# Mamba layer: y summed by channels on TensorE, dt read from its bank, six of sixteen states' dt·u·B made by TensorE

## The chip, the cores and the metric

One core of one Trainium2 chip runs the whole program. The time is device microseconds of one execution; runs agree within some 0.5%, and the kernel before was timed three times. The engines are TensorE (PE, with its weight loads in a row of their own, PEld), VectorE (DVE), ScalarE (ACT), GpSimd (POOL) and SyncE (SP, which only issues DMAs here). Each engine works through its own instructions in order and waits on semaphores that the others count up.

## The reference, cut to what matters

The program is one layer: a bidirectional Mamba block over 8 sequences of 512 tokens with 128 model channels, then attention and a mixture of experts. Only the Mamba block is touched. For each sequence and each of the two directions (256 inner channels, 16 states):

```
u, z = split(x @ Win.T);  u = silu(conv4(u) + convb)
dtr, B, C = split(u @ Wx.T)                     # 8, 16, 16 wide
dt = softplus(dtr @ Wdt.T + bdt)
h[n] = exp(dt * A[n]) * h[n] + (dt * u) * B[n]  # over 512 tokens, for each of 16 states n
y = sum over n of h[n] * C[n]  + u * D
out = (y * silu(z)) @ Wout.T
```

The backward direction runs the same on the flipped sequence and flips the result.

## The kernel before, in words

Everything of the scan lies by channels: 128 channels on the partitions, 512 tokens in the free dimension, so that the 256 channels are two halves h = 0, 1. One (sequence b, direction d) is a unit: 16 units in a row, written as a first unit, a loop over pairs of units (d = 1 of a sequence, then d = 0 of the next) and a last unit. A unit has 32 steps s, with state n = s // 2 and half h = s % 2. At each step:

- ACT makes `da = exp(dt * A[n])` into a ring of 8 (`act_da`, L722).
- DVE multiplies `dtu = dt*u` with the row B[n] spread over the partitions, which TensorE puts into a bank of `bp` by a bf16 matmul (`pe_b`, L479): `dbu`, L866. Then it scans (`dve_scan`, L882).
- POOL multiplies the scanned row with C[n] spread over the partitions: `hc`, L1025, a ring of 8.
- TensorE adds it up (`pe_y`, L491): four transposes of 128x128 add the 512 tokens of `hc` into `yp`, which lies by tokens. The same happens once for u·D (`ud`).

For four states of a unit (`BY_PE`) TensorE makes dtu·B itself, by matmuls of the transposed dtu (`pe_dtt`, L440, copied by ACT into `dtt`) with diagonal matrices of B, which ACT writes (`act_diag`, L690): `pe_fill`, L454, one call for each half. The scan then reads that bank.

While a unit scans, the other work of its neighbours is done in the same steps. The front of the next unit: the convolution as 8 matmuls (`pe_u`, L402), z (`pe_z`, L411), Wx (`pe_xd`, L420), Wdt (`pe_dt`, L470), B transposed (`pe_bt`, L428), softplus on ACT as Abs, Relu, Exp, Ln (L702 to L710) and the sum on DVE (`dve_dt`, L852), then dtu (L857). The tail of the unit before: the last five `pe_y`, then y·silu(z) on DVE (`dve_yg`, L889), TensorE transposes that back to channels (`pe_ygt`, L508), ACT copies it (`act_ygt`, L730), and Wout follows once for both directions (`pe_out`, L514), with its end on DVE (L897 to L911).

The order on each engine is written out by hand: `pe_unit`, `act_unit`, `dve_unit` and `pool_unit` run over s and call what is due. A "slot s" of TensorE below is one turn of the loop in `pe_unit`: in odd slots the B row or the first half's fill of state s//2 + 1, in even slots the second half's fill of state s//2 - 1, then the y of step s - 5 (`LAG_Y`), then tail and front. A unit with direction 1 carries the tail of direction 0 and has no `pe_out`; it is called A here. A unit with direction 0 carries the tail of direction 1 with `pe_out`; it is called B.

After the 16 units (at about 990 us) attention and experts run in a part of the program that is left as it was.

Of the kernel before, what the change touches and what calls it, by code (L numbers as in the profile page):

```python
# [18 lines left out]
ALU = mybir.AluOpType  # L19
# [57 lines left out]

FIRST_IN = (2, 4)
# [12 lines left out]
BY_PE = ((2, 4, 12, 14), (2, 4, 6, 14))  # L91
N_PE = len(BY_PE[0])
DIAG_AT = ((-1, 5, 18, 20), (-1, 5, 11, 20))
# [20 lines left out]
def mamba_phase(nc, sems, shared, x, x1, cscr, w, ffn):  # L114

    with ExitStack() as ctx:
# [30 lines left out]
        sz = part(NDIR, TC, DI)  # L147
        yg = part(TC, DI)
# [11 lines left out]
        eps = shared["wt"][:, taken:taken + TC]  # L160
        q9, k9 = shared["q9"], shared["k9"]
# [6 lines left out]
        ncol = sb("ncol", [P, 2])  # L168
# [37 lines left out]
        lnw = ncol  # L206
# [41 lines left out]
        ygt_ready = sig("ygt_ready", 4, "tensor")  # L248
# [20 lines left out]
        dt_done = sig("dt_done", 4, "vector")  # L269
# [17 lines left out]
                   (late_loaded, wu[:, 1], w["tap_w"][:, 1]), (late_loaded, wout[...], w["wout"]))  # L287

# [12 lines left out]
        def sp_first_load(sp):  # L301
# [9 lines left out]
            sp.dma_start(lnw[:, :], ffn["lnw"]).then_inc(ffn_loaded, 16)  # L311
# [77 lines left out]
        def pe_u(pe, b, d, i, first=False):  # L389
# [53 lines left out]
        def pe_fill(pe, b, d, n, h):  # L443
# [9 lines left out]
            for c in range(TC):  # L453
                last = nc.tensor.matmul(dst[:, c * P:(c + 1) * P], dtt[:, c, h * P:(h + 1) * P], diag[:, (N_PE * d + e) % 2, c, :],  # L454
# [26 lines left out]
        def pe_y(pe, b, d, s):  # L481
# [14 lines left out]
        def pe_ygt(pe, b, d, last_unit=False):  # L496
            pe.wait_ge(yg_done, count(yg_done, b, d + 1))
            if last_unit:
                pe.wait_ge(ygt_done, count(ygt_done, b, 2))
                pe.wait_ge(res_done, count(res_done, b, 0))  # L500
                pe.wait_ge(first_rope, 4)
            elif d:
                pe.wait_ge(dtt_done, count(dtt_done, b + 1, 2))
            else:
                pe.wait_ge(dtt_done, count(dtt_done, b, 4))
            for h in range(NH2):
                for c in range(TC):
                    last = nc.tensor.transpose(wp[:, h, c * P:(c + 1) * P], yg[:, c, h * P:(h + 1) * P], ident[:, :])  # L508
                last.then_inc(ygt_ready, 1)

        def pe_out(pe, b, c):
            pe.wait_ge(ygt_done, count(ygt_done, b, 4))
# [18 lines left out]
        def pe_unit(pe, b, d, front=None, tail=None, after=None):  # L531


            for s in range(STEPS):
# [21 lines left out]
                if tail and s == 7:  # L556
                    pe_ygt(pe, *tail)
# [8 lines left out]
                if front:  # L566
# [18 lines left out]
        def _(pe):  # L585
# [58 lines left out]
        def act_silu_z(act, b, d, k):  # L644
            act.wait_ge(z_ready, count(z_ready, b, 2 * d + k + 1))
            if k == 0:
                act.wait_ge(yg_done, count(yg_done, b, d - 1))
            h = k ^ d
            nc.scalar.activation(sz[:, d, 2 * h:2 * h + 2, :], wp[:, h, :].rearrange("p (c n) -> p c n", c=2),
                                 ACT.Silu).then_inc(silu_done, 1)  # L650

        def act_xd(act, b, d, k):
# [5 lines left out]
            elif k == 1:  # L658
# [4 lines left out]
                nc.scalar.activation(xd[:, :], wp[:, d, :], ACT.Copy).then_inc(xd_done, 1)  # L663
# [2039 lines left out]
```

## Time and profile before

| | us |
|---|---|
| three runs | 1722.72, 1725.72, 1731.79; median 1725.72 |
| the profiled execution | 1706.65, span 1704.9 |
| Mamba part | first scan at 38.9, last scan at 976.6 |
| DVE busy over the span | 1385.4 (81%) |
| PE busy over the span | 1323.4 (78%) |
| POOL, ACT busy over the span | 1109.9 (65%), 1062.2 (62%) |

Busy shares are means over the Mamba part and the part behind it. A row of a timeline gives start, duration, engine, line, operation, tiles and shapes, how many instructions stand in the row, and in brackets the idle time before it with what ended it. A matmul's duration holds its pipeline's tail, so what one costs TensorE in a dense stretch is the distance from its start to the start of the next row. One matmul of the program in f32 leaves two records, one f32 transpose of 128x128 leaves one.

### The profile page before, as it was taken

Reading aid. Unit: us, or ns where it says so; the run is one execution under the profiler, and the core shown is the slowest. Engines: PE = TensorE matmul, PEld = TensorE weight load, DVE = VectorE, ACT = ScalarE, POOL = GpSimd, SP = SyncE. Lnnn points to the kernel's source line nnn. Section 1 sums busy time; section 2 is a strip of 40 time slices with the busy share of each in tenths; the row PEclk is TensorE's granted clock in tenths of the full one; section 3 lists DMA queues with packets and bytes.
Section 4 is the critical chain, followed back from the end, with each engine's and each line's share of the span. In section 5 each row is a group of like instructions: output and inputs, shape, how many; then the busy total and the mean of one; then the engine's idle time right before and its main releaser. Section 6 shows DMA issues by size and latency. Waiting matters only on the chain. (4 is left out here: it accounts for less than half of the span.)

```text
span 1704.9 us, 30907 instructions
## 1 busy us (share of the span) xinstructions
PE 1323.4 (78%) x8880; PEld 958.7 (56%) x8880; DVE 1385.4 (81%) x2234; ACT 1062.2 (62%) x1888; POOL 1109.9 (65%) x1244
## 2 busy tenths in 40 slices
PE   4877788787778777877877658888988888888771
PEld 2656566566656665665666433335665556656671
DVE  2999999999999999999999846676778777777432
ACT  6777777776786776777867315565665656556330
POOL 1777777787877777777868814444557566655535
PEclk8989998899889899898998757898999999999886
DMA  5112302320321123023203021134556455564662
GB/s 190 54 59 101 125 1 99 124 99 4 121 99 61 64 99 124 0 99 124 81 19 141 27 89 30 50 125 134 175 152 200 149 173 168 155 198 134 224 221 72
DMA packets 115274, 186.05 MB, mean 109 GB/s; under 512 B 10736, under 2 KB 87536, under 8 KB 110960
## 3 DMA queue, kind: packets, MB, share of 16 engines
q1 hardware_dynamic: 111056, 176.30, 29.9%
q0 software_dynamic: 4096, 8.40, 1.7%
q8 instruction: 44, 0.72, 0.2%
q14 instruction: 78, 0.64, 0.1%
HBM read 153.92 MB, written 26.15 MB: 106 GB/s over the span
## 5 line engine op out<-in xcount | busy, mean ns | idle before, releaser
L882 DVE TENSOR_TENSOR_SCAN wt<-da,dbu 128x512 f32<-128x512 f32 x448 | 527.6, 1204 | 17.4 <-ACT da L722 6.8
L722 ACT ACTIVATE da<-dt,a_neg 128x512 f32<-128x512 f32 x512 | 351.4, 716 | 186.2 <-DVE wt L882 161.4
L1025 POOL TENSOR_TENSOR hc<-wt,qk 128x512 f32<-128x512 f32 x256 | 327.8, 1299 | 97.2 <-DVE wt L882 75.3
L1025 POOL TENSOR_TENSOR hc<-wt,cb 128x512 f32<-128x512 f32 x256 | 326.1, 1294 | 93.0 <-DVE wt L882 87.9
L491 PE MATMUL yp<-ident,hc 128*128 128x128 f32 x2048 | 321.8, 291 | 5.4 <-POOL hc L1025 5.1
L2018 ACT ACTIVATE pt<-scores,lift 128x512 f32<-128x512 f32 x320 | 216.3, 684 | 167.3 <-PE scores L1761 165.8
L491 PEld LDWEIGHTS yp<-ident,hc 128*128 128x128 f32 x2048 | 271.9, 153 | 84.6 <-issue 52.2
L2149 DVE TENSOR_REDUCE mx<-wp 128x1 f32<-128x384 f32 (+3 forms) x352 | 217.9, 635 | 91.3 <-PE wp L1723 86.9
L866 DVE TENSOR_TENSOR dbu<-dtu,bp 128x512 f32<-128x512 f32 x384 | 251.4, 684 | 10.9 <-PE bp L479 1.0
L2496 POOL TENSOR_SCALAR_AFFINE_SELECT pt<-pt 128x256 f32<-128x256 f32 (+1 forms) x320 | 119.0, 375 | 190.1 <-ACT pt L2018 189.0
L402 PE MATMUL wp<-xpad,wu 128*128 128x512 f32 x256 | 132.5, 610 | 11.6 <-DVE wt L897 6.5
L1723 PE MATMUL wp<-qk 72*128 72x384 bf16 (+3 forms) x512 | 136.1, 324 | 0.0
L1761 PE MATMUL scores<-qk 75*128 75x384 bf16 (+3 forms) x512 | 130.6, 317 | 3.4 <-ACT pt L2018 3.4
L1720 PE MATMUL wp<-mask,identb 128*128 128x128 bf16 (+2 forms) x352 | 91.3, 259 | 32.5 <-DVE mx L2149 26.5
L1780 PE MATMUL og<-pt,vpad 128*32 128x512 f32 (+3 forms) x1024 | 98.3, 482 | 23.0 <-POOL pt L2496 23.0
L440 PE MATMUL wp<-ident,dtu 128*128 128x128 f32 x128 | 31.5, 427 | 79.7 <-DVE dtu L857 79.7
L2516 POOL DMA_INDIRECT yk<-ys_scratch,pos_e x64 | 61.8, 966 | 45.6 <-DMA ys_scratch<-ysb 30.7
L479 PE MATMUL bp<-st,sel 96*128 96x512 bf16 x192 | 78.8, 410 | 10.3 <-DVE dbu L866 9.6
L1761 PEld LDWEIGHTS scores<-qk 75*128 75x128 bf16 x512 | 48.7, 102 | 64.0 <-ACT pt L2018 32.1
L454 PE MATMUL dbu<-diag,wt 128*128 128x128 f32 x512 | 71.1, 282 | 16.4 <-DVE wt L882 16.4
L454 PEld LDWEIGHTS dbu<-diag,wt 128*128 128x128 f32 x512 | 64.4, 193 | 33.3 <-DVE wt L882 26.0
L690 ACT ACTIVATE diag<-ident,bt 128x128 f32<-128x128 f32 x256 | 81.2, 389 | 1.6
(252 smaller groups left out, 2441.9 us busy)
## 6 DMA issues: line engine op xcount, KB each, us to landing
wt<-ffn_w_e SPq DMA_DIRECT2D x120, 384.0 KB, 4.4
qk<-c_scratch SPq DMA_DIRECT2D x8, 3072.0 KB, 11.6
cb<-c_scratch SPq DMA_DIRECT2D x8, 3072.0 KB, 11.8
qk<-q_scratch SPq DMA_DIRECT2D x96, 96.0 KB
qk<-c_scratch SPq DMA_DIRECT2D x8, 1024.0 KB, 4.7
cb<-c_scratch SPq DMA_DIRECT2D x8, 1024.0 KB, 4.7
xg<-xs_scratch SPq DMA_DIRECT2D x24, 256.0 KB, 3.4
ys_scratch<-ysb SPq DMA_DIRECT2D x24, 256.0 KB, 3.0
```

Source lines behind the costliest of these rows:

```text
L402: last = nc.tensor.matmul(wp[:, h, :], wu[:, d, j, h * P:(h + 1) * P], xpad[:, d, j:j + SEQ], start=(j == 0), stop=(j == NTAP - 1))
L454: last = nc.tensor.matmul(dst[:, c * P:(c + 1) * P], dtt[:, c, h * P:(h + 1) * P], diag[:, (N_PE * d + e) % 2, c, :], start=True, stop=True)
L491: last = nc.tensor.matmul(yp[:, c, h * P:(h + 1) * P], src[:, c * P:(c + 1) * P], ident[:, :], is_transpose=True, start=(s < 0 and h == 0 ...
L722: nc.scalar.activation(da[:, s % NDA, :], dt[:, h, :], ACT.Exp, scale=a_neg[:, d, h, n:n + 1]).then_inc(da_done, 1)
L866: nc.vector.tensor_tensor(dbu[:, dbu_bank(d, n) ^ h, :], dtu[:, h, :], bp[:, n % 2, :], ALU.mult).then_inc(dbu_done, 1)
L882: nc.vector.tensor_tensor_scan(hb[:, s % NHB, :], da[:, s % NDA, :], src, 0.0, ALU.mult, ALU.add).then_inc(scan_done, 1)
L1025: nc.gpsimd.tensor_tensor(hc[:, s % NHC, :], hb[:, s % NHB, :], cb[d][:, s // 2, :], ALU.mult).then_inc(hc_done, 1)
L1723: last = nc.tensor.matmul(heads[:, i, :], q9[0:PART_ROWS, at, h0_ % GH + i, c * P:(c + 1) * P], k9[0:PART_ROWS, at, 0:width], start=False, ...
L1761: last = nc.tensor.matmul(sp_[:, t % 2, at:at + SEQ - kc * P], k9[:, group, kc * P:(kc + 1) * P], q9[:, group, h % GH, kc * P:], start=Tru ...
L2018: nc.scalar.activation(pt[:, (ST_TILES * b + t) % NPR, 0:width], scores_in, ACT.Exp, bias=lift[:, :], scale=SCALE).then_inc(exp_done, 1)
L2149: nc.vector.reduce_max(mx[:, c, h:h + n], ms[:, t % 2, 0:n * (c + 1) * P].rearrange("p (n k) -> p n k", n=n), mybir.AxisListType.X).then_i ...
L2496: nc.gpsimd.affine_select(out=found, in_=found, pattern=[[0, len(pieces(t))], [1, P]], base=0, channel_multiplier=-1, compare_op=ALU.is_ge ...
```

## The change

Five things are done together.

1. `yp` now lies by channels. `pe_y` is one f32 matmul of 512 columns with the identity as weights, in place of four transposes; `dve_yg` writes `ygt` directly (for direction 1 backwards), and `pe_ygt` and `act_ygt` go. `sz` lies by channels too, for which `pe_z` is one matmul of 512 columns per half in place of two of 256.
2. `BY_PE` has six states in both directions (2, 4, 6, 8, 12, 14) in place of four, with four buffers of diagonals in place of two and the diagonals written at other steps.
3. The bias of dt comes with the matmul, by a row of ones in `xd`; ACT's Relu goes, and DVE makes max(., 0) + ln(.) of each half straight from the bank, in steps 28 and 29.
4. B is transposed in slot 24 between the two `pe_dt`, not in slot 30, and copied in ACT's step 29.
5. Waits follow these edits; those on `ygt_done` become waits on `dtt_done` or `yg_done`.

```
-BY_PE = ((2, 4, 12, 14), (2, 4, 6, 14))
+BY_PE = ((2, 4, 6, 8, 12, 14), (2, 4, 6, 8, 12, 14))
...
-DIAG_AT = ((-1, 5, 18, 20), (-1, 5, 11, 20))
+DIAG_AT = ((-1, 4, 8, 12, 17, 21), (-1, 4, 8, 12, 17, 21))
...
+        yp = shared["yp"][:, :, :].rearrange("p c n -> p (c n)").rearrange("p (h s) -> p h s", h=NH2)
...
         def pe_z(pe, b, d, k):
             pe.wait_ge(silu_done, count(silu_done, b, 4 * d + k + 1))
             h = k ^ d
-            for c in (2 * h, 2 * h + 1):
-                last = nc.tensor.matmul(wp[:, h, (c % 2) * DI:(c % 2 + 1) * DI],
-                                        xpad[:, d, NTAP - 1 + c * P:NTAP - 1 + (c + 1) * P], win_z[:, d, :],
-                                        start=True, stop=True)
-            last.then_inc(z_ready, 1)
+            nc.tensor.matmul(wp[:, h, :], win_z[:, d, h * P:(h + 1) * P], xpad[:, d, NTAP - 1:NTAP - 1 + SEQ],
+                             start=True, stop=True).then_inc(z_ready, 1)
...
         def pe_dt(pe, b, d, h):
...
+            else:
+                pe.wait_ge(bt_done, count(bt_done, b, d + 1))
...
             for h in (range(NH2) if s < 0 else (s % 2,)):
                 src = ud[:, h, :] if s < 0 else hc[:, s % NHC, :]
-                for c in range(TC):
-                    last = nc.tensor.matmul(yp[:, c, h * P:(h + 1) * P], src[:, c * P:(c + 1) * P], ident[:, :],
-                                            is_transpose=True, start=(s < 0 and h == 0 and c % 2 == 0),
-                                            stop=(s == STEPS - 1), skip_group_check=True)
+                last = nc.tensor.matmul(yp[:, h, :], ident[:, :], src, start=(s < 0), stop=(s >= STEPS - NH2),
+                                        skip_group_check=True)
             last.then_inc(y_added, 1)
...
-                if tail and s == 7:
-                    pe_ygt(pe, *tail)
...
-            act.wait_ge(fill_done, count(fill_done, b, N_PE * d + e - 1))
+            act.wait_ge(fill_done, count(fill_done, b, N_PE * d + e - 3))
...
-                nc.scalar.activation(t_relu[:, h, :], wp[:, 1 - (h ^ d), :], ACT.Relu, bias=bias).then_inc(soft_done, 1)
...
-                nc.vector.tensor_tensor(dt[:, :, :], t_ln[:, :, :], t_relu[:, :, :], ALU.add).then_inc(dt_done, 1)
...
+                nc.vector.scalar_tensor_tensor(dt[:, k, :], wp[:, 1 - (k ^ d), :], 0.0, t_ln[:, k, :],
+                                               ALU.max, ALU.add).then_inc(dt_done, 1)
...
-            dve.wait_ge(ygt_ready, count(ygt_ready, b, 2 * d))
-            nc.vector.tensor_tensor(yg[:, :, :], yp[:, :, :], sz[:, d], ALU.mult).then_inc(yg_done, 1)
+            dve.wait_ge(out_ready, count(out_ready, b, 0))
+            out = ygt[:, d]
+            nc.vector.tensor_tensor(out[:, :, ::-1] if d else out, yp, sz[:, d], ALU.mult).then_inc(yg_done, 1)
```

TensorE, first unit (direction 0), from the work on state 6 in slot 11 on. `bp<-st,sel` is a B row, `bp<-diag,wt` or `dbu<-diag,wt` a fill, `wp<-xpad,wu` the convolution, `yp` the sum over states. Before:

```order
L479 MATMUL bp<-st,sel 128x512
L491 MATMUL yp<-ident,hc 128x128 x8
L402 MATMUL wp<-xpad,wu 128x512
L479 MATMUL bp<-st,sel 128x512
L491 MATMUL yp<-ident,hc 128x128 x4
L402 MATMUL wp<-xpad,wu 128x512
L491 MATMUL yp<-ident,hc 128x128 x4
L402 MATMUL wp<-xpad,wu 128x512
L479 MATMUL bp<-st,sel 128x512
L491 MATMUL yp<-ident,hc 128x128 x4
```

The same place of the same engine now:

```order
L455 MATMUL bp<-wt 128x128 x4
L493 MATMUL yp<-hc,ident 128x512 x2
L407 MATMUL wp<-xpad,wu 128x512
L482 MATMUL bp<-st,sel 128x512
L493 MATMUL yp<-hc,ident 128x512
L407 MATMUL wp<-xpad,wu 128x512
L455 MATMUL dbu<-wt 128x128 x4
L493 MATMUL yp<-hc,ident 128x512
L407 MATMUL wp<-xpad,wu 128x512
L455 MATMUL bp<-wt 128x128 x4
L493 MATMUL yp<-hc,ident 128x512
L407 MATMUL wp<-xpad,wu 128x512 x2
```

The B rows of states 6 and 8 have become two fills each, and each group of four transposes is one matmul of 512 columns.

DVE, first unit, from the first scan of state 4 to state 9. `L882` and `L862` are the scans (the listing names them by their instruction's class), `L866` and `L846` the products. Before:

```order
L882 SCALAR_TENSOR_TENSOR wt<-da,bp 128x512
L866 TENSOR_TENSOR dbu<-dtu,bp 128x512
L882 SCALAR_TENSOR_TENSOR wt<-da,dbu 128x512
L866 TENSOR_TENSOR dbu<-dtu,bp 128x512
L882 SCALAR_TENSOR_TENSOR wt<-da,dbu 128x512 x2
L866 TENSOR_TENSOR dbu<-dtu,bp 128x512 x2
L882 SCALAR_TENSOR_TENSOR wt<-da,dbu 128x512 x2
L866 TENSOR_TENSOR dbu<-dtu,bp 128x512 x2
```

Now:

```order
L862 SCALAR_TENSOR_TENSOR wt<-da,bp 128x512
L846 TENSOR_TENSOR dbu<-dtu,bp 128x512
L862 SCALAR_TENSOR_TENSOR wt<-da,dbu 128x512
L846 TENSOR_TENSOR dbu<-dtu,bp 128x512
L862 SCALAR_TENSOR_TENSOR wt<-da,dbu 128x512 x2
L862 SCALAR_TENSOR_TENSOR wt<-da,bp 128x512
L846 TENSOR_TENSOR dbu<-dtu,bp 128x512
L862 SCALAR_TENSOR_TENSOR wt<-da,dbu 128x512
L846 TENSOR_TENSOR dbu<-dtu,bp 128x512
```

The pair of products for state 6 is gone from DVE, its scan reads the bank that TensorE filled, and the products of state 7 stand singly behind its two scans.

## Rows read from the trace of the kernel before

**Rows 1.** Windows, 100 us: busy of each engine, granted clock, DMA.
```profile
200.00:300.00 100.00, 78.71 (x480) 62.23 (x479) 97.79 (x114) 73.62 (x137) 75.95 (x63) 0.88 0.20 81
```
**Rows 2.** Timeline, DVE: dtu at the end of three units.
```profile
266.98 1.19 DVE L857 TENSOR_TENSOR dtu<-dt,u 128x1024 f32<-128x1024 f32 x1
...
327.30 1.19 DVE L857 TENSOR_TENSOR dtu<-dt,u 128x1024 f32<-128x1024 f32 x1
...
385.14 1.19 DVE L857 TENSOR_TENSOR dtu<-dt,u 128x1024 f32<-128x1024 f32 x1
```
**Rows 3.** Timeline, DVE: the B unit between the first two of these.
```profile
283.18 1.19 DVE L882 TENSOR_TENSOR_SCAN wt<-da,bp 128x512 f32<-128x512 f32 x1
...
285.08 1.21 DVE L882 TENSOR_TENSOR_SCAN wt<-da,dbu 128x512 f32<-128x512 f32 x1
...
289.17 1.27 DVE L866 TENSOR_TENSOR dbu<-dtu,bp 128x512 f32<-128x512 f32 x2
...
292.59 1.27 DVE L866 TENSOR_TENSOR dbu<-dtu,bp 128x512 f32<-128x512 f32 x2
...
300.33 1.19 DVE L882 TENSOR_TENSOR_SCAN wt<-da,dbu 128x512 f32<-128x512 f32 x1
...
303.74 1.35 DVE L911 TENSOR_SCALAR wt<-wt 128x128 f32<-128x128 f32 x4
...
316.48 1.22 DVE L882 TENSOR_TENSOR_SCAN wt<-da,dbu 128x512 f32<-128x512 f32 x1 [1.51 <-ACT da L722]
...
324.34 1.91 DVE L852 TENSOR_TENSOR dt<-t_ln,t_relu 128x1024 f32<-128x1024 f32 x1
326.17 1.21 DVE L882 TENSOR_TENSOR_SCAN wt<-da,dbu 128x512 f32<-128x512 f32 x1
```
**Rows 4.** Timeline, PE: the same unit.
```profile
268.22 1.97 PE L440 MATMUL wp<-ident,dtu 128*128 128x128 f32 x8 [4.52 <-DVE dtu L857]
...
277.39 1.06 PE L491 MATMUL yp<-ident,ud 128*128 128x128 f32 x8 [0.76 <-DVE wt L889]
...
282.03 0.60 PE L491 MATMUL yp<-ident,hc 128*128 128x128 f32 x4
282.47 1.06 PE L454 MATMUL dbu<-diag,wt 128*128 128x128 f32 x8
283.36 0.60 PE L491 MATMUL yp<-ident,hc 128*128 128x128 f32 x4
...
288.43 1.02 PE L402 MATMUL wp<-xpad,wu 128*128 128x512 f32 x2
289.29 0.38 PE L479 MATMUL bp<-st,sel 96*128 96x512 bf16 x1
289.51 0.60 PE L491 MATMUL yp<-ident,hc 128*128 128x128 f32 x4
...
304.33 1.49 PE L411 MATMUL wp<-win_z,xpad 128*128 128x256 f32 x4 [2.81 <-ACT u L642]
```
**Rows 5.** The page, costliest groups: the convolution and the sum over states.
```profile
L491 PE MATMUL yp<-ident,hc 128*128 128x128 f32 x2048 | 321.8, 291 | 5.4 <-POOL hc L1025 5.1
L402 PE MATMUL wp<-xpad,wu 128*128 128x512 f32 x256 | 132.5, 610 | 11.6 <-DVE wt L897 6.5
```
**Rows 6.** Timeline, ACT: the same unit, the table load for silu, and silu.
```profile
302.29 1.28 ACT L642 ACT_TABLE_LOAD   x1
303.59 1.26 ACT L642 ACTIVATE u<-wp,col 128x512 f32<-128x512 f32 x2
```
**Rows 7.** Windows, 2 us, the same unit: columns as in rows 1.
```profile
266.00:268.00 2.00, 0.00 (x0) 0.00 (x0) 2.00 (x2) 1.96 (x4) 0.79 (x1) 0.50 0.16 66
...
274.00:276.00 2.00, 2.00 (x18) 1.96 (x17) 2.00 (x2) 1.99 (x4) 1.10 (x2) 0.94 0.00 0
...
306.00:308.00 2.00, 2.00 (x8) 1.61 (x7) 2.00 (x4) 0.45 (x1) 2.00 (x3) 0.50 0.21 63
```
**Rows 8.** Instructions of the tile yp, experts part: minimum/median/maximum ns.
```profile
L2301 DVE SCALAR_TENSOR_TENSOR ga<-th,yp x48: 535/682/689, 1168.9 to 1597.6; 128x512 f32<-128x512 f32 x36, 128x384 f32<-128x384 f32 x12
```

More of the change, by code:

```diff
@@ L75, in is_first @@
     return isinstance(b, int) and b == 0
+ONE_ROW = DT_ROW + DTR
 FIRST_IN = (2, 4)
@@ L145, in part @@
             return a.rearrange(f"p ({names}) -> p {names}", **dict(zip("abcd", shape)))
-        sz = part(NDIR, TC, DI)
-        yg = part(TC, DI)
+        sz = part(NDIR, NH2, SEQ)
         ygt = part(NDIR, NH2, SEQ)
@@ L160, in mamba_phase @@
         eps = shared["wt"][:, taken:taken + TC]
+        taken += TC
+        diag_more = part(2, TC, P)
         q9, k9 = shared["q9"], shared["k9"]
@@ L453, in pe_fill @@
             for c in range(TC):
-                last = nc.tensor.matmul(dst[:, c * P:(c + 1) * P], dtt[:, c, h * P:(h + 1) * P], diag[:, (N_PE * d + e) % 2, c, :],
+                last = nc.tensor.matmul(dst[:, c * P:(c + 1) * P], dtt[:, c, h * P:(h + 1) * P], diag_of(d, e)[:, c, :],
                                         start=True, stop=True)
@@ L489, in pe_y, with pe_out @@
                 src = ud[:, h, :] if s < 0 else hc[:, s % NHC, :]
-                for c in range(TC):
-                    last = nc.tensor.matmul(yp[:, c, h * P:(h + 1) * P], src[:, c * P:(c + 1) * P], ident[:, :],
-                                            is_transpose=True, start=(s < 0 and h == 0 and c % 2 == 0),
-                                            stop=(s == STEPS - 1), skip_group_check=True)
+                last = nc.tensor.matmul(yp[:, h, :], ident[:, :], src, start=(s < 0), stop=(s >= STEPS - NH2),
+                                        skip_group_check=True)
             last.then_inc(y_added, 1)
[L496 to L499, printed above, removed]
-                pe.wait_ge(res_done, count(res_done, b, 0))
[L501 to L512, printed above, removed]
+        def pe_out(pe, b, c, last_unit=False):
+            if c == 0:
+                pe.wait_ge(yg_done, count(yg_done, b, 2))
+                if last_unit:
+                    pe.wait_ge(first_rope, 4)
+                    pe.wait_ge(dtt_done, count(dtt_done, b, 4))
+                else:
+                    pe.wait_ge(dtt_done, count(dtt_done, b + 1, 2))
+                pe.wait_ge(res_done, count(res_done, b, 0))
             for k in range(NDIR * NH2):
@@ L575, in pe_unit @@
                         pe_xd(pe, *front)
-                    if s == 30:
-                        pe_bt(pe, *front)
                     if s in (24, 25):
                         pe_dt(pe, *front, s - 24)
+                    if s == 24:
+                        pe_bt(pe, *front)
             if not after:
@@ L662, in act_xd @@
                 act.wait_ge(bt_ready, count(bt_ready, b, d))
-                nc.scalar.activation(xd[:, :], wp[:, d, :], ACT.Copy).then_inc(xd_done, 1)
+                nc.scalar.activation(xd[:, :], wp[:, d, :], ACT.Identity, bias=ncol[:, 2:3]).then_inc(xd_done, 1)
             elif k == 2:
@@ L723, in act_da @@
                                  scale=a_neg[:, d, h, n:n + 1]).then_inc(da_done, 1)
-        def act_ygt(act, b, d, h):
-            act.wait_ge(ygt_ready, count(ygt_ready, b, 2 * d + h + 1))
-            if h == 0:
-                act.wait_ge(out_ready, count(out_ready, b, 0))
-            out = ygt[:, d, h, :]
-            nc.scalar.activation(out[:, ::-1] if d else out, wp[:, h, :], ACT.Copy).then_inc(ygt_done, 1)
         def act_front(act, b, d, at, first=False):
@@ L750, in act_front @@
                     act.preload_act_table_set("natural_log_exp_and_others")
+            if at == 29:
+                act_bt(act, b, d)
             if at == STEPS - 1:
                 for h in range(NH2):
-                    for k in range(4):
+                    for k in range(3):
                         act_soft(act, b, d, h, k)
@@ L796, in act_unit @@
                         act_diag(act, b, d, e)
-                if tail and s in (14, 15):
-                    act_ygt(act, *tail, s - 14)
                 if front:
@@ L957, in dve_unit @@
                         dve_first_rope(dve, k)
-                if front and s in (29, 30):
-                    dve_dt(dve, *front, s - 29)
+                if front and s in (28, 29, 30):
+                    dve_dt(dve, *front, s - 28)
         @block.vector
```

78 lines of the change are left out of this document (37 added, 41 removed).

## The prediction

> **What bounds the kernel now.** I read the busy shares by stage first. In 100 us of the Mamba part DVE is busy 97.8 us, PE 78.7, POOL 76.0, ACT 73.6 [rows 1]: DVE sets the pace, and the wish is to take work off it. Then the unit: from dtu to dtu a B unit takes 60.32 us and the A unit behind it 57.84, so a pair takes 118.16 [rows 2]. Then the timelines of DVE and PE inside one B unit [rows 3, 4], since the change moves work from DVE to PE and PE's share is not a small one. DVE hardly waits there: once 1.51 us for ACT's da. PE does wait, 4.52 us for dtu and 2.81 us for silu; but between these two its rows stand close together, and that is where the change adds most.
>
> **DVE, what goes.** A state made by TensorE together with the next, DVE-made one takes 283.18 to 289.17, 5.99 us; a state made by DVE takes 289.17 to 292.59, 3.42 us, so two take 6.84 [rows 3]. Each state moved saves 0.85 us (not the whole pair of products: behind a TensorE-made state the next products stand singly and wait for the scan ahead). Two per unit: 1.7. The sum for dt takes 324.34 to 326.17, 1.83 us [rows 3]; two reads of a bank with max and add, 0.68 us each [rows 8], are 1.36: 0.5 saved. Reading the bank could cost half as much again or as little as the products do; that is ±0.5 a unit and stays in the range. Writing y·silu(z) backwards in direction 1 has no row on DVE; I take 0, at most another 1.2 us in every second unit, and if the new dense rows help, 0.3 less. Saved per unit: 2.2 us. Without any wait of DVE a B unit would be 60.32 - 1.51 - 2.2 = 56.6 us, an A unit 57.84 - 2.2 = 55.6.
>
> **PE, what comes.** The four transposes of one y occupy PE from 282.03 to 282.47, 0.44 us [rows 4]. One f32 matmul of 512 columns, two records, occupies it from 288.43 to 289.29, 0.86 us [rows 4]; the counts bear this out, 256 records for the 128 convolution matmuls of 16 units, 2048 for 16 x 32 x 4 transposes [rows 5]. Both are at the full clock. So each y costs 0.42 us more, 34 times a unit (32 and the two of u·D): +14.3. A fill of one half takes 0.89 us (282.47 to 283.36), a B row 0.22 (289.29 to 289.51) [rows 4]: two more states are 4 fills for 2 B rows, +3.1. The transposition of gated rows goes, 8 records like a fill: -0.9. z is the same number of columns. The sum for a B unit now: y 34 x 0.86 = 29.2; 12 fills 10.7; 10 B rows 2.2; convolution, z, Wx, Wdt, 14 x 0.86 = 12.0; transposes of dtu and B 1.3; Wout, four pieces of 8 records, 3.6: 59.1 us. An A unit has no Wout and 0.4 for x: 56.0. The first lies 2.5 above what DVE needs (56.6), the second level with it (55.6). PE becomes the engine with the most work, and has to wait for others besides.
>
> A rule of the Trainium skill prices this otherwise: "TensorE: Matmul & The Clock Gate", section Terms, says of the transpose mode that it is four times faster for FP32; by that a y as a matmul would cost 4 x 0.44 = 1.76 us. The rows above show 0.86, a factor of two, and the measured one is used.
>
> **Where it is felt.** PE takes its slots in order, and a scan of a TensorE-made state waits for the fill ahead of it. So each stretch between two such fills takes the longer of the two engines' times. Four stretches of a B unit:
>
> - *From y·silu(z) to scan 9.* PE then has u·D (2 matmuls), y0 to y4, two fills and a B row ahead: 7 x 0.86 + 2 x 0.89 + 0.22 = 8.0. DVE's steps take 277.39 to 285.08, 7.7 [rows 3, 4]. Late by 0.3.
> - *From scan 9 to scan 17.* PE has 8 y, 7 convolution matmuls, 4 fills, 2 B rows and the 4 pieces of Wout: 15 x 0.86 + 8 x 0.89 + 0.44 = 20.5. DVE took 285.08 to 300.33, 15.25 [rows 3], and one and a half moved states take 1.25 off: 14.0. DVE waits 6.5. This is the largest term: the front's convolution and four of the fills fall in the same eight steps, and PE comes in without any lead (the stretch before).
> - *From scan 17 to scan 25.* PE does y13, the last convolution, a B row and y14 in 2.8 and then stands before z, which waits for silu: scan 17, one da (1.2 + 0.6), a table load of 1.28 and silu of 0.6 [rows 6], 3.8. Behind it 12 matmuls of 0.86 (2 z, 6 y, 2 Wx, 2 Wdt), 2 fills, 2 B rows and B's transposes (0.44): 13.0, together 16.8. DVE: 300.33 to 316.48 less the stall of 1.51 is 14.6, and half a moved state less is 14.2. It waits 2.6. The old stall for da goes, since DVE is late by then and ACT is ahead.
> - *Around dtu.* PE runs out of work some 3.9 us before dtu is there (by the same sums; 4.52 before), so the clock is at its lower level, 1.2 GHz, when it goes on: before, the granted clock was 0.50 at 266 to 268 and back at 0.94 only in 274 to 276, six us after the work began [rows 4, 7]. Transposes of dtu, y27 and y28 take 2 x 2.6 = 5.2 cold, and the B row of state 1 comes behind them, at 5.5 after dtu; DVE wants it after one scan, a pair of products and two scans, 4.6. It waits 0.9.
>
> So B: 56.6 + 0.3 + 6.5 + 2.6 + 0.9 = 66.9, 6.6 more than now. In an A unit PE has 3.2 less in the second stretch. DVE also has less there: 285.08 to 292.59 is free of tail work, 7.51, and one more state and two thirds of another (3.42 + 2.3) make 13.2 of the 15.25; 2.05 are the tail's [rows 3]. So it waits 5.3. In the third stretch DVE lacks L911's 1.3 [rows 3] and waits 3.9. A: 55.6 + 0.3 + 5.3 + 3.9 + 0.9 = 66.0, 8.2 more. As a check from the other side: PE's 59.1 and 56.0 with 3.9 + 1.0 idle and 2.6 lost to the clock are 66.6 and 63.5.
>
> Seven pairs: 7 x 14.8 = 104. The first unit has neither tail nor transposes of x: +4.9 + 3.9 - 2.2 = +6.6. The last has no front: -2.2 + 0.3 + 0.9 = -1. At the program's start two Relu of about 0.6 leave the chain: -1. At its end five y cost 2.1 more, the transposes and copies of the last gated rows 2.1 less: 0. ACT's two more states of diagonals are hidden: it is busy 74% now, loses two Relu and two copies a unit, and DVE gives it time; if that cover were gone, it would be some 2 us a unit. The experts' part stays. Total +108.
>
> The profiled execution took 1706.65 us, so it would take 1815; the median of the runs shown is 19 us above it, 1725.72, which gives **1834 us**.
>
> **Rivals.**
>
> 1. *PE hides it, DVE stays the bound (faster).* Pairs of 112.2 or, since PE's own sum is 115.1, PE-bound without any idling: 118.16 - 115.1 = 3.1 a pair, 7 pairs and the ends -22 to -27: about 1700. For it: PE is idle a fifth of the stretch now. Against it: it needs under 1.5 us of waiting of PE per unit, and dtu and silu alone give it 5. It decides from the point where PE can enter slot 10 with some 6 us of lead; the wait of u·D for y·silu(z), 277.39, allows none. 7%, of which 1% ends within the limit of no change.
> 2. *Half hidden.* The y are not needed by DVE at once, and a lead that I have missed (POOL's products stand ready earlier in the slowed steps, the ring of 8) takes up half of the waits: +54, 1780. 16%, 3% of it down to no change.
> 3. *Colder.* One more idle stretch of PE per unit falls as it did before z, where 2.81 idle left a clock of 0.50 in 306 to 308 [rows 4, 7]; 3 us of work at the lower level cost 3 more in each unit: +48, 1882. For it: PE waits for y·silu(z) too. Against: the wait at z shrinks to 1.0. 11%.
> 4. *A y costs 1.76 us.* An f32 matmul with the identity would have to run at half the rate of the convolution's, which has the same form; 34 x 0.9 = 30 us more per unit, about 2310. 1%.
>
> The skill's factor of four, named above, is what the fourth rival would be.
>
> My forecast has the remaining 65%. The range is **1765 to 1890**: below it lie the first rival and the lower part of the second, above it the cold case with every unknown at its dear end. A measurement of this kernel tells about 0.5%, 9 us, from no change: faster 0.06, no change 0.04, slower 0.90.
>
> **What would show it.** In the new profile: PE's busy share in the Mamba part above 90%, DVE's down to about 85%; the y rows 64 + 4 records a unit at 0.43 us apart; scans whose idle time is ended by the fill (L455), about 6 us together in steps 9 to 17 and 3 to 4 in step 25; dtu to dtu 65 to 68 us; PE's idle before z down to about 1 us. It would be wrong if the scans' waits for fills stay under 3 us a unit, if y's matmuls stand closer than 0.8 us apart, or if the scans wait for da or POOL instead.

## The result and the profile after

The changed kernel takes 1851.78 us against 1724.22 us for the one before: a ratio of 1.0743 with a 95% interval of 1.0691 to 1.0795. It is slower, as forecast, by 127.6 us where 108 were forecast; 1834 lies 18 us too low. One execution of 8474.75 us is left out; the others took 1844 to 1853. The profiled one took 1853.36 us.

The page of the kernel after, three of its costliest groups (the columns of [rows 5]):

```profile
L862 DVE TENSOR_TENSOR_SCAN wt<-da,dbu 128x512 f32<-128x512 f32 x416 | 492.4, 1208 | 109.4 <-PE dbu L455 77.8
L493 PE MATMUL yp<-hc,ident 128*128 128x512 f32 x1024 | 534.6, 622 | 2.2 <-POOL hc L1007 1.9
L846 DVE TENSOR_TENSOR dbu<-dtu,bp 128x512 f32<-128x512 f32 x320 | 215.3, 691 | 85.4 <-PE bp L482 73.9
```

The sum over states has 1024 records for 2048 but takes 534.6 us for 321.8 [rows 5]. The scans now wait 109.4 us, 77.8 of it for the second half of a state that TensorE makes, and the products wait 85.4 us, 73.9 of it for a B row.

Windows of the kernel after (the columns of [rows 1]):

```profile
200.00:300.00 100.00, 89.92 (x324) 48.30 (x322) 80.63 (x103) 66.35 (x122) 68.83 (x59) 0.97 0.24 96
300.00:310.00 10.00, 6.19 (x15) 3.64 (x16) 8.45 (x11) 7.63 (x15) 7.12 (x5) 0.66 0.01 2
310.00:371.00 61.00, 56.34 (x233) 32.61 (x231) 49.34 (x63) 35.02 (x65) 39.73 (x33) 1.00 0.23 87
```

Against [rows 1] PE went from 78.7 to 89.9 us in 100 and DVE from 97.8 to 80.6. The two engines have changed places. The second row is the stretch around dtu, the only one of this unit at a lowered clock.

DVE's timeline of the kernel after, the B unit that answers to [rows 3], with every wait over 0.3 us:

```profile
302.37 1.20 DVE L837 TENSOR_TENSOR dtu<-dt,u 128x1024 f32<-128x1024 f32 x1
...
309.63 1.29 DVE L846 TENSOR_TENSOR dbu<-dtu,bp 128x512 f32<-128x512 f32 x2 [1.51 <-PE bp L482]
...
323.11 1.22 DVE L862 TENSOR_TENSOR_SCAN wt<-da,dbu 128x512 f32<-128x512 f32 x1 [0.66 <-PE dbu L455]
...
330.18 0.70 DVE L846 TENSOR_TENSOR dbu<-dtu,bp 128x512 f32<-128x512 f32 x1 [1.78 <-PE bp L482]
333.84 1.22 DVE L862 TENSOR_TENSOR_SCAN wt<-da,dbu 128x512 f32<-128x512 f32 x1 [2.96 <-PE dbu L455]
...
343.58 1.22 DVE L862 TENSOR_TENSOR_SCAN wt<-da,dbu 128x512 f32<-128x512 f32 x1 [1.61 <-PE dbu L455]
...
358.26 0.70 DVE L846 TENSOR_TENSOR dbu<-dtu,bp 128x512 f32<-128x512 f32 x1 [1.54 <-PE bp L482]
361.03 1.22 DVE L862 TENSOR_TENSOR_SCAN wt<-da,dbu 128x512 f32<-128x512 f32 x1 [2.07 <-ACT da L709]
...
371.21 1.20 DVE L837 TENSOR_TENSOR dtu<-dt,u 128x1024 f32<-128x1024 f32 x1
```

The unit takes 68.84 us where 60.32 stood [rows 2]. Its seven waits add up to 12.13 us; a short one for DVE's own result is 0.28; without them 56.4 are left, DVE's own work. The scans at 323.11, 343.58 and 361.03 are scans 9, 17 and 25, the ends of the forecast's stretches.

PE's timeline of the kernel after, from scan 17 to scan 25:

```profile
343.22 1.02 PE L493 MATMUL yp<-hc,ident 128*128 128x512 f32 x2
344.08 1.02 PE L407 MATMUL wp<-xpad,wu 128*128 128x512 f32 x2
344.94 0.38 PE L482 MATMUL bp<-st,sel 96*128 96x512 bf16 x1
345.16 1.02 PE L493 MATMUL yp<-hc,ident 128*128 128x512 f32 x2
347.61 1.13 PE L415 MATMUL wp<-xpad,win_z 128*128 128x512 f32 x2 [1.43 <-ACT u L633]
...
358.93 1.02 PE L473 MATMUL wp<-xd,wdt 128*128 128x512 f32 x2
359.78 1.05 PE L455 MATMUL dbu<-diag,wt 128*128 128x128 f32 x8
```

A y at 343.22 occupies PE for 0.86 us, as the convolution's matmul at 344.08. PE stands once, 1.43 us before z (2.81 before [rows 4]), and between 347.61 and the fill at 359.78 without a gap. The fill occupies PE until 360.67; scan 25 starts at 361.03. That is 0.36 us later, as at scans 9 and 17 (slot's end 322.75, scan 323.11; 343.22 and 343.58). The label of scan 25's wait names ACT's da, but the scan did not wait for it. ACT's rows of the kernel after:

```profile
344.83 0.72 ACT L709 ACTIVATE da<-dt,a_neg 128x512 f32<-128x512 f32 x1 [3.19 <-DVE wt L862]
...
360.17 0.70 ACT L709 ACTIVATE da<-dt,a_neg 128x512 f32<-128x512 f32 x1
```

The first is the da of step 25, which ACT makes just ahead of silu; the second, which ended at 360.87, is that of step 31. What scan 25 waited for is PE's fill.

The same is true of the wait of 1.51 us in the kernel before, which the prediction reads as one for ACT's da [rows 3]. PE's and ACT's rows there:

```profile
315.23 1.05 PE L454 MATMUL dbu<-diag,wt 128*128 128x128 f32 x8
316.12 0.60 PE L491 MATMUL yp<-ident,hc 128*128 128x128 f32 x4
...
301.55 0.72 ACT L722 ACTIVATE da<-dt,a_neg 128x512 f32<-128x512 f32 x1 [0.65 <-DVE wt L882]
...
315.73 0.70 ACT L722 ACTIVATE da<-dt,a_neg 128x512 f32<-128x512 f32 x1
```

The da of step 25 ran at 301.55. The fill held PE until 316.12, and the scan started at 316.48, again 0.36 later. So that unit of the kernel before was already late by PE's work behind z.

### The profile page after: what moved, and what is told of

Same layout as the page of the kernel before. It is cut to its first block and busy times, and to the rows that moved or that the text cites. A ratio compares the mean times of both kernels' runs of the same rounds, so it can differ in the third digit from the quotient of the medians.

```text
span 1851.6 us, 29301 instructions
## 1 busy us (share of the span) xinstructions
PE 1562.2 (84%) x8080; PEld 931.6 (50%) x8080; DVE 1349.9 (73%) x2186; ACT 1069.5 (58%) x1952; POOL 1111.4 (60%) x1244
## 5 line engine op out<-in xcount | busy, mean ns | idle before, releaser
L862 DVE TENSOR_TENSOR_SCAN wt<-da,dbu 128x512 f32<-128x512 f32 x416 | 492.4, 1208 | 109.4 <-PE dbu L455 77.8
L493 PE MATMUL yp<-hc,ident 128*128 128x512 f32 x1024 | 534.6, 622 | 2.2 <-POOL hc L1007 1.9
L846 DVE TENSOR_TENSOR dbu<-dtu,bp 128x512 f32<-128x512 f32 x320 | 215.3, 691 | 85.4 <-PE bp L482 73.9
L493 PEld LDWEIGHTS yp<-hc,ident 128*128 128x128 f32 x1024 | 189.2, 201 | 147.9 <-issue 107.2
L862 DVE TENSOR_TENSOR_SCAN wt<-da,bp 128x512 f32<-128x512 f32 x96 | 115.3, 1202 | 7.3 <-PE bp L455 5.1
L407 PEld LDWEIGHTS wp<-xpad,wu 128*128 128x128 f32 x256 | 47.8, 194 | 66.1 <-issue 51.5
L2486 POOL DMA_INDIRECT xs_scratch<-h2n,posi x64 | 64.3, 1005 | 24.2 <-issue 10.8
L1700 PEld LDWEIGHTS wp<-mask,identb 128*128 128x128 bf16 x352 | 36.1, 103 | 68.4 <-DVE mx L2129 28.3
```

Source lines behind the costliest of these rows:

```text
L407: last = nc.tensor.matmul(wp[:, h, :], wu[:, d, j, h * P:(h + 1) * P], xpad[:, d, j:j + SEQ], start=(j == 0), stop=(j == NTAP - 1))
L493: last = nc.tensor.matmul(yp[:, h, :], ident[:, :], src, start=(s < 0), stop=(s >= STEPS - NH2), skip_group_check=True)
L846: nc.vector.tensor_tensor(dbu[:, dbu_bank(d, n) ^ h, :], dtu[:, h, :], bp[:, n % 2, :], ALU.mult).then_inc(dbu_done, 1)
L862: nc.vector.tensor_tensor_scan(hb[:, s % NHB, :], da[:, s % NDA, :], src, 0.0, ALU.mult, ALU.add).then_inc(scan_done, 1)
L1700: nc.tensor.matmul(heads[:, :, c * P:width], identb[:, :], mask[:, :].unsqueeze(1).to_broadcast([P, n, P]), start=True, stop=False, skip_g ...
```

## The experiments

The theory under test: VectorE waits because TensorE, in order, has more to do between two fills of TensorE-made states than VectorE has between the scans that need them; what a matmul costs depends on the stretch in which it stands. The main rival: TensorE's total load sets the time, wherever it stands. Each ratio is against the kernel before, run on the same chip; "over the kernel before" below is the distance to that run, 128 us for the change itself. "y" is the accumulation of one scan's gated rows.

**1. Half of each y** (changed kernel; half of the columns of the 32 y of a unit are not computed).

```diff
-last = nc.tensor.matmul(yp[:, h, :], ident[:, :], src, ...
+w = SEQ if s < 0 else SEQ // 2
+last = nc.tensor.matmul(yp[:, h, 0:w], ident[:, :], src[:, 0:w], ...
```

> The changed kernel, but each of the 32 y matmuls of a unit sums only the first 256 of the 512 tokens (the rest of y is left out, it keeps only u*D); order, waits, fills and diagonals stay. Theory (TensorE's columns for y are the cost): a y falls from 0.86 to 0.43 us, so the stretch from scan 9 to 17 of a B unit needs 17.1 us of TensorE in place of 20.5, the one to scan 25 some 14.2 in place of 16.8, and units fall from 68.8 and 67.7 to about 58 and 57: 1690 us (1675 to 1715). Rival 1 (the two more states, their fills and diagonals are the cost): these are untouched, 1835 to 1855. Rival 2 (the cold stretch around dtu): the cold y27 and y28 halve, 20 to 30 us less, about 1825.

Measured: 1757.42 us, 1.022 [1.0154, 1.0285]. It is 38 us over the kernel before, so some 90 us come back and not the 162 that the theory, as put here, had said. With y as cheap on PE as before, VectorE still waits. Groups of DVE from 100 to 900 us in this run:

```profile
L863 DVE TENSOR_TENSOR_SCAN wt<-da,dbu 128x512 f32<-128x512 f32 x335 | 396.4, 1207 | 61.6 <-PE dbu L455 55.6 <-POOL hc L1008 3.3 <-DVE wt L818 1.5
L847 DVE TENSOR_TENSOR dbu<-dtu,bp 128x512 f32<-128x512 f32 x256 | 172.1, 690 | 29.7 <-PE bp L482 20.1 <-DVE wt L863 1.4
```

So the rate of y is not the whole of it; six states have a price of their own.

**2. Four states** (changed kernel with the states of before).

```diff
-BY_PE = ((2, 4, 6, 8, 12, 14), (2, 4, 6, 8, 12, 14))
-DIAG_AT = ((-1, 4, 8, 12, 17, 21), (-1, 4, 8, 12, 17, 21))
+BY_PE = ((2, 4, 12, 14), (2, 4, 6, 14))
+DIAG_AT = ((-1, 5, 18, 20), (-1, 5, 11, 20))
```

> The changed kernel with the old table of four states and the old steps of the diagonals; y by matmul and dt from the bank stay. Theory: TensorE has 3.1 us less in a unit, DVE 1.7 more; B 68.8 to 66.1, A 67.7 to 64.8: about 1810 us (1790 to 1830). Rival 1 (fills and diagonals are the cost): back to the old kernel or a little under, 1710 to 1730.

Measured: 1748.49 us, 1.0174 [1.0112, 1.0236]. This is nearer to the rival than to the theory as I had put it, and outside both ranges: y by channels costs some 30 us by itself. My forecast had taken PE's and DVE's totals and not the stretches. In a B unit of this run no fill stands between scan 9 and scan 25, and DVE's waits for PE there are these two:

```profile
326.37 0.70 DVE L846 TENSOR_TENSOR dbu<-dtu,bp 128x512 f32<-128x512 f32 x1 [0.87 <-PE bp L482]
...
329.14 1.22 DVE L862 TENSOR_TENSOR_SCAN wt<-da,dbu 128x512 f32<-128x512 f32 x1 [2.07 <-PE dbu L455]
```

They are 2.9 us, against 10.0 in the same place of the changed kernel: with 3.1 us of PE's work, 7 us of waits went.

**3. y by transposes** (the kernel before with the other three parts: six states, dt from the bank, the bias in its matmul).

```diff
-BY_PE = ((2, 4, 12, 14), (2, 4, 6, 14))
+BY_PE = ((2, 4, 6, 8, 12, 14), (2, 4, 6, 8, 12, 14))
-nc.vector.tensor_tensor(dt[:, :, :], t_ln[:, :, :], t_relu[:, :, :], ALU.add)
+nc.vector.scalar_tensor_tensor(dt[:, k, :], wp[:, 1 - (k ^ d), :], 0.0, t_ln[:, k, :], ALU.max, ALU.add)
```

> The old kernel with parts 2 to 4 of the change (six states, dt from the bank, B transposed between the two dt matmuls) and without part 1: y by four transposes, gated rows transposed back; three buffers of diagonals in place of four for want of room. Theory: TensorE has about 45 us of work in a unit and DVE stays the bound; 2.2 us less per unit and part of the old stall for da: 1680 us (1670 to 1700), faster than both. Rival 1 (fills or diagonals are the cost, or ACT becomes late by them): 1724 or more.

Measured: 1767.26 us, 1.0283 [1.0219, 1.0346]. A clear miss: I had expected a gain. In that kernel PE is busy only 647 of 800 us, and yet DVE waits; its timeline in a B unit:

```profile
303.95 1.22 DVE L890 TENSOR_TENSOR_SCAN wt<-da,dbu 128x512 f32<-128x512 f32 x1 [2.46 <-PE dbu L461]
...
312.69 1.22 DVE L890 TENSOR_TENSOR_SCAN wt<-da,dbu 128x512 f32<-128x512 f32 x1 [0.61 <-PE dbu L461]
...
327.04 0.69 DVE L874 TENSOR_TENSOR dbu<-dtu,bp 128x512 f32<-128x512 f32 x1 [1.09 <-PE bp L488]
329.39 1.22 DVE L890 TENSOR_TENSOR_SCAN wt<-da,dbu 128x512 f32<-128x512 f32 x1 [1.65 <-PE dbu L461]
```

The forecast's second stretch has 20.5 us of PE's work; with eight y cheaper by 0.42 it is 17.1, against DVE's 14.0. The difference is 3.1 us, and the first two waits are 2.46 + 0.61 = 3.07. That the two agree so closely is partly chance. PE did have a lead of 1.4 us at scan 9 (its fill's slot ended at 293.69, the scan started at 295.41), and lost it by 1.55 us of standing and starting again: 0.60 us for ACT's copy of the gated rows, 0.42 until DVE had read the result of Wout. The A units lose more than the B units, 64.1 us for 57.8; there PE also stands 1.63 us for the padded rows of the front (see experiment 6).

**4. Six states alone** (the kernel before with the tables of experiment 3 and a third buffer for diagonals).

> The old kernel with part 2 alone: six states, three buffers of diagonals, the new steps of the diagonals. Theory of the stretches: the fills of states 6 and 8 fall in the slots of the convolution; with y at 0.44 a B unit has 17.1 us of TensorE from scan 9 to scan 17 against 14.0 of DVE, so it waits 3.1 there and more at scan 25, which is more than the 1.7 saved: 1750 to 1780. Rival (as above): 1700, what DVE saves.

Measured: 1771.35 us, 1.0281 [1.0212, 1.0349], as expected. The six states alone cost 48 to 50 us, although each takes products off VectorE. In a B unit the waits in the second stretch are 2.45 + 0.61 us, as forecast; but the larger part of the loss lies in the A units (64.1 us for 57.8; B 62.3 for 59.4 to 60.3), where PE stands 1.63 us for the padded rows, which the theory had not foreseen.

**5. dt alone** (the kernel before with dt from the bank and the bias in its matmul).

> The old kernel with parts 3 and 4 alone: dt read from its bank, no Relu, B transposed between the two dt matmuls; the old four states, y by transposes. Theory: 0.5 to 0.6 us less of DVE in a unit and two Relu less on ACT ahead of the old stall for da: 8 to 16 us less, 1705 to 1716. Rival (B's transposes and the wait for their copy, now ahead of the second dt matmul and the fill of state 12, are what made the kernel with y by tokens slow): 1740 or more.

Measured: 1717.32 us, 0.9959 [0.9917, 1.0001]. At most a small gain, just outside the 1705 to 1716 forecast: these two parts are not the cause. The forecast leaned on the old stall for da, which was one for PE's fill; in this run it has not gone (a B unit):

```profile
437.02 1.22 DVE L887 TENSOR_TENSOR_SCAN wt<-da,dbu 128x512 f32<-128x512 f32 x1 [1.65 <-PE dbu L458]
```

**6. and 7. Less y in one place** (changed kernel; of the y of four steps only 16 columns are computed, in the steps 6 to 9 and in the steps 23 to 26).

```diff
+w = 16 if s in (6, 7, 8, 9) else SEQ        # and (23, 24, 25, 26)
```

> The changed kernel, but the y matmuls of steps 6 to 9 sum only 16 of the 512 columns (the rest of these four products is left out of y). They stand in slots 11 to 14 of TensorE, between the fills that release scan 9 and scan 17; 4 x 0.83 = 3.3 us of TensorE's work goes from that stretch. Theory (each stretch between two fills takes the longer of TensorE's and DVE's time): DVE's wait there, 6.4 us, shrinks one for one: 3.3 x 15 = 50 us less, about 1800. Rival (what counts is TensorE's total, wherever it lies): also 50 less. Rival (the fills themselves or the diagonals are late): 1850.

> The same cut in steps 23 to 26, whose y stand in slots 28 to 31: the same 3.3 us of TensorE's work per unit goes, but from the place ahead of its wait for dtu. Theory of the stretches: nothing is gained, TensorE only waits longer for dtu (7.7 us in place of 4.4): 1845 to 1860. Rival (TensorE's total): about 1800, as in the other.

Measured: 1832.21 us, 1.0655 [1.06, 1.0711], for the steps 6 to 9, and 1847.49 us, 1.0762 [1.0705, 1.0818], for 23 to 26. The same 2.85 us of PE's work a unit was cut (3.3 had been reckoned). At the end it brings nothing, as expected, and the rival, which gives both the same, is out. In the middle 50 us were expected, and some 15 to 20 came, so the theory of the two engines alone is not enough. The B units became 2.5 us shorter on average (66.3 for 68.8), nearly one for one, but the A units not at all (67.7 as before the cut). PE's and ACT's timelines in such an A unit:

```profile
386.32 0.52 PE L494 MATMUL yp<-hc,ident 128*128 128x16 f32 x4
388.99 2.07 PE L407 MATMUL wp<-xpad,wu 128*128 128x512 f32 x2 [2.15 <-ACT xpad L621]
...
387.00 1.27 ACT L681 ACTIVATE wt<-ident,bt 128x128 f32<-128x128 f32 x4
388.17 0.76 ACT L621 ACTIVATE xpad<-wp,ncol 128x512 f32<-128x512 f32 x1
```

PE now stands 2.15 us for the front's padded rows (0.78 in the changed kernel). Behind that the granted clock is 0.75 from 388 to 390 and 0.50 from 390 to 392, and the four rows from 388.99 on take 1.85 us more than the same matmuls at 1.00. So the time saved is lost to the next thing that PE needs and to the clock. ACT makes the padded rows in two halves, in steps 16 and 17, and the change has it write diagonals in step 17 too, ahead of the second half: 1.27 us at 387.00.

**8. A warm clock** (changed kernel with 18 small matmuls, whose result isn't used, ahead of the transposition of dtu).

```diff
+pe.wait_ge(dt_done, count(dt_done, b, 3 * d + 1))
+for _ in range(18):
+    nc.tensor.matmul(wp[:, 1 - d, 0:P], ident[:, :], ident[:, :], start=True, stop=True)
```

> The changed kernel with 18 small f32 matmuls of the identity with itself (128 columns, into a part of the bank that the transposes of dtu then overwrite) put ahead of the transposes of dtu, once dt of the first half is read: TensorE is then busy while it waits for dtu. Theory: the clock stays at 2.4 GHz, the wait of 1.5 us for the B row of state 1 goes in nearly every unit, 15 to 25 us less, about 1830; the waits for fills in the middle stay. Rival 2 (the cold stretch is the main cost): 60 us less or more, under 1790. If the clock does not follow: 1850.

Measured: 1832.04 us, 1.0669 [1.0603, 1.0735], as expected. From 100 to 900 us the granted clock is 1.00 for 0.95. In the B units the wait for the B row of state 1 is gone (67.0 us for 68.8). The cold stretch around dtu is worth 15 to 20 us (113 over the kernel before for 128), not the 127.

**9. The six states moved** (changed kernel; only the places of the states and of their diagonals differ).

```diff
-BY_PE = ((2, 4, 6, 8, 12, 14), (2, 4, 6, 8, 12, 14))
-DIAG_AT = ((-1, 4, 8, 12, 17, 21), (-1, 4, 8, 12, 17, 21))
+BY_PE = ((2, 3, 4, 5, 13, 14), (2, 3, 4, 5, 13, 14))
+DIAG_AT = ((-1, 3, 4, 6, 20, 22), (-1, 3, 4, 6, 20, 22))
```

> The changed kernel whole, with the six states in other slots: 2, 3, 4, 5, 13, 14 in place of 2, 4, 6, 8, 12, 14, so that no fill stands from slot 13 to slot 24, where convolution, z and Wx stand. TensorE's total is the same to the instruction. Stretch theory: scans 12 to 26 then carry some 26 us of TensorE against 28 of VectorE and wait little; scans 4 to 11 carry 8 fills and 10 rows of y, about 18 us against 13, and wait some 5 us; the end some 2. Unit about 65 against 68.3: 1800 (1775 to 1825). Rival (TensorE's total load, 90% of the stretch, sets the time wherever fills stand): 1840 to 1860.

Measured: 1795.62 us, 1.0449 [1.0398, 1.0501]; the theory had said 1800, the rival 1840 to 1860. The matmuls are the same in number and form, and 50 to 56 us are gone (78 over the kernel before for 128). DVE's timeline, a B unit:

```profile
289.25 1.20 DVE L837 TENSOR_TENSOR dtu<-dt,u 128x1024 f32<-128x1024 f32 x1
...
296.51 1.29 DVE L846 TENSOR_TENSOR dbu<-dtu,bp 128x512 f32<-128x512 f32 x2 [1.51 <-PE bp L482]
...
308.19 1.22 DVE L862 TENSOR_TENSOR_SCAN wt<-da,dbu 128x512 f32<-128x512 f32 x1 [3.30 <-PE dbu L455]
...
311.69 1.22 DVE L862 TENSOR_TENSOR_SCAN wt<-da,dbu 128x512 f32<-128x512 f32 x1 [1.17 <-PE dbu L455]
...
316.30 1.22 DVE L862 TENSOR_TENSOR_SCAN wt<-da,dbu 128x512 f32<-128x512 f32 x1 [1.48 <-PE dbu L455]
...
348.28 1.22 DVE L862 TENSOR_TENSOR_SCAN wt<-da,dbu 128x512 f32<-128x512 f32 x1 [2.87 <-PE dbu L455]
...
355.50 1.20 DVE L837 TENSOR_TENSOR dtu<-dt,u 128x1024 f32<-128x1024 f32 x1
```

Three waits of 5.95 us stand where the states 2 to 5 are made (5 were expected), one of 2.87 at the end (2 were expected), and from 316.30 to 348.28, where convolution, z and Wx stand, none is over 0.3. The wait of 1.51 us behind dtu is what it was. The unit takes 66.25 us for 68.84.

Two things qualify this run. The diagonals moved with the states, so that none stands between the two halves of the padded rows any more; the A units (63.1 us for 67.7) may owe about 1 us of their gain to that. And PE now stands only before dtu: from 301.73 on it has no gap in this unit. Its work of 59.1 us (the prediction's sum), 4.08 us of idling and 3.0 us that the matmuls behind dtu take longer at the lower clock make 66.1 of the 66.25 us. So PE's own sum is the limit here, and even without any idling it is about as long as a B unit of the kernel before (59.4 to 60.3): by this sum, another place for the six fills won't make the change pay by itself.

**10. and 11. Five states** (the kernel before with state 3 added in both directions and a third buffer for diagonals; then the same with dt from the bank and the bias in its matmul).

```diff
-BY_PE = ((2, 4, 12, 14), (2, 4, 6, 14))
+BY_PE = ((2, 3, 4, 12, 14), (2, 3, 4, 6, 14))
```

> The kernel before with a fifth state (3) made by TensorE, its two fills in the slots 5 and 8, where no front stands; a third diagonal buffer; y and dt as before. Stretch theory (a fill costs where front work stands between it and the next fill, and little elsewhere): each unit loses two products of VectorE (some 1.5 us) and gains two fills of 0.89 between scans 4 and 9, where TensorE then has about 9 us (six fills, eight transposed rows, the transposition of a tail) against 7.5 of VectorE's six scans: 0.7 to 1.5 us of waits come back. Units 0 to 0.8 us shorter: 1700 to 1722, likeliest 1710. Rival (a fill more costs wherever it stands, as six states did: +50 for two more, so +25 for one): 1740 to 1750.

> The same five states with dt from the bank and the bias in its matmul (parts 3 and 4 of the change). Those two parts alone gave 1717.32 against 1721.19. By the stretch theory the two gains add: 1696 to 1718, likeliest 1706, the fastest so far. Rival: with VectorE's softplus shorter TensorE is later by as much, and nothing is added: as the run with five states alone.

Measured: 1736.2 us, 1.0116 [1.007, 1.0162], and 1727.19 us, 1.0049 [1.0018, 1.0079]. Both missed: I had hoped for a version faster than both kernels. The fifth state alone costs 18 us over the kernel before, near the 25 of the first rival; with the dt parts it is 9. DVE's and PE's timelines with five states alone, at the start of a unit:

```profile
290.85 1.22 DVE L889 TENSOR_TENSOR_SCAN wt<-da,dbu 128x512 f32<-128x512 f32 x1 [2.03 <-PE dbu L461]
```

```profile
276.45 1.97 PE L447 MATMUL wp<-ident,dtu 128*128 128x128 f32 x8 [4.51 <-DVE dtu L864]
...
285.62 1.06 PE L498 MATMUL yp<-ident,ud 128*128 128x128 f32 x8 [0.66 <-DVE wt L896]
...
289.60 1.06 PE L461 MATMUL dbu<-diag,wt 128*128 128x128 f32 x8
```

I had taken slots 5 and 8 for light ones, because no front stands there. But PE comes to them from 4.51 us of idling, and from 276.45 to the fill that the scan needs, at 289.60 to 290.49, it stands only once, 0.66 us. That stretch was nearly full without the fifth state: before, the slot of the fill for scan 9 ends at 283.36 [rows 4] and the scan starts at 285.08 [rows 3], which leaves 1.4 us beside the 0.36 that lie between the two anyhow. The fifth state adds two fills for a B row, 1.56 us, and its scan comes two steps earlier. The scan's wait of 2.03 us is more than the 1.5 that two products would have saved. No version tried beats the kernel before clearly; dt alone comes nearest.

## Why the prediction was right, point by point

- *VectorE's own work.* Forecast 56.6 us for a B unit without waits, measured 56.4 (56.7 with the short wait of 0.28, which the forecast's 60.32 holds too). Right.
- *The old stall.* The prediction takes DVE's 1.51 us as a wait for ACT's da that goes because ACT will be ahead. This reading was wrong: it was PE's fill (above). The sum is not harmed, since it takes the 1.51 off and lets PE's work set the third stretch; but the row was an early sign that PE set it already.
- *A y is 0.86 us of PE, 0.42 more.* Right, by the PE rows above, and the fourth rival is out. The Trainium skill ("TensorE: Matmul & The Clock Gate", section Terms) calls the transpose mode four times faster for FP32; here it is 0.86 over 0.44, a factor of two, and the measurement decides.
- *First stretch, to scan 9.* Forecast 0.3, measured 0.66. PE's 8.0 us are right (314.67 to 322.75); what the sum left out is the 0.36 us from the end of the fill's slot to the scan.
- *Second stretch, scan 9 to scan 17.* Forecast 20.5 us on PE and a wait of 6.5; measured 343.58 - 323.11 = 20.47, and 1.78 + 2.96 + 1.61 = 6.35. Right, the term that carried the forecast. In the A unit behind it (371.21 to 438.93, 67.72 us) the waits there are 0.58 + 2.07 + 1.67 + 2.07 = 6.4 where 5.3 were forecast: PE stands 0.78 for the padded rows of the front, a wait that I had not looked for, and that experiment 6 showed growing when y is cut. PE's and ACT's rows of that unit:

```profile
395.43 1.26 ACT L680 ACTIVATE wt<-ident,bt 128x128 f32<-128x128 f32 x4
396.60 0.76 ACT L620 ACTIVATE xpad<-wp,ncol 128x512 f32<-128x512 f32 x1
...
397.41 1.12 PE L407 MATMUL wp<-xpad,wu 128*128 128x512 f32 x2 [0.78 <-ACT xpad L620]
```

PE was through with its y at 396.47 and lost 0.94 us, and 0.11 more on the first matmul: 1.05, the whole difference. By these rows the padded rows would have been ready at 396.1 without the diagonals at 395.43 (an estimate; no run moves only these). So the term that the prediction put at nothing, ACT's diagonals being hidden, was about 1 us in each A unit.
- *Third stretch, scan 17 to scan 25.* Forecast 16.8 us and a wait of 2.6; measured 17.45 and 1.54 + 2.07 = 3.6; in the A unit 4.5 for 3.9. PE's idle before z is 1.43 where I had 1.0: z starts 4.03 us after scan 17, where the forecast has 3.8 (its own terms add up to 3.7). The work behind it takes 13.06 for 13.0, the 0.36 to the scan comes on top, and DVE's own work is 13.8 for 14.2; together that is the 1.0 us.
- *Around dtu.* Forecast 0.9, measured 1.51 in the B unit and 0.76 in the A unit. PE idles 4.43 us before it (3.9 forecast) and the clock is 0.66 over the ten microseconds around it. Experiment 8 shows that the cause is the clock.

So the mechanism stands, and four terms were sized too low by 0.4 to 1.1 us. Of the signs named ahead, PE's busy share is 89.9% (above 90 was named), DVE's 80.6% (85), dtu to dtu is 67.7 to 68.8 us (65 to 68). A pair of units takes 68.84 + 67.72 = 136.6 us where 132.9 were forecast: 3.7 a pair, 26 us over seven pairs. In the profiled executions the last product y·silu(z) moved from 990.98 to 1128.87 us, 138 later, against 108. That the medians moved by 128 only, and the forecast is 18 off and not 30, is luck: the profiled execution of before lay 19 us under its median, that of after at its median.

The second rival (a lead takes up half of the waits) is refuted by the result: the waits of the second stretch came in full, 6.35 for 6.5. In experiment 3, with PE busy 81%, a lead of 1.4 us did come up at scan 9, and was lost to PE's own waits on the way to scan 17. The third (a colder clock) went the other way, 0.95 against 0.91 from 100 to 900 us, while PE is busy 718 of these 800 us for 632. Of the parts, six states alone cost 48 to 50 us, y by channels alone (with the dt parts) some 30, dt alone nothing; together 127. They are not additive: in the second stretch of a B unit DVE waits for PE not at all with y by channels alone (experiment 2), 3.06 us with six states alone (experiment 4) and 6.35 us with both.

What stays open is whether the change can be made to pay. Experiment 9 moved the fills out of the front's steps, and what was left is PE's own work with its idling and lower clock around dtu; work for PE in that place was not tried, nor were the front's own steps or the diagonals of step 17 moved by themselves.

## What to carry to other kernels

Where an engine works in order and another waits for some of its results, cut the program at those results and add up both engines' work between two cuts; the longer one counts in each stretch, and idle time in another stretch is no help. A step of a third engine that the first must wait for inside a stretch, as the padded rows here, belongs in the sum. A busy share of 79% can hide a stretch with nothing to spare, so before adding work look at which stretch it falls in, and at what holds the engine just ahead of it. Work moved to an engine that idles a fifth of the time may still lose, as the fifth state did. And check the engine that a wait names against the step whose result was needed: the name was wrong for scan 25 before and after.

## What the runs showed of the hardware

- A transposition of 512 f32 columns takes 0.44 us and a plain f32 matmul of 512 columns 0.86, at the same granted clock; so adding up by transposes is the cheaper of the two, although TensorE then loads weights 2048 times for the sum over states and not 1024.
- Behind 4.43 us without work on PE the granted clock was 0.50 from 304 to 308 us, the level of 1.2 GHz, and eight transposes took 1.73 us there, where four take 0.44 at 1.00; 18 small matmuls ahead of them kept the clock at 1.00 and gave 15 to 20 us in the whole program, although they add work.
- From the end of a fill's slot on PE to the start of the scan that reads it pass 0.36 us, at scans 9, 17 and 25 alike.
- The wait that a row names need not be the one that made it late: scan 25 names ACT's da, although the da that it reads was done 15 us earlier, while the fill behind 13 us of PE without a gap ended its slot 0.36 us ahead of it.
